# Two fused transformer layers: expert addresses in three VectorE steps with PSUM scratch, unread identity matmuls, and a refitted time table

## The reference, cut to what matters

```python
x  = L0_attn_x                                   # (8, 512, 128)
xn = _layernorm(x)
x  = x + L0_attn(xn) + L0_ffn(xn)                # causal, 16 heads of 8, keys from a latent of 32; routed experts
xn = _layernorm(x)
x  = x + L1_attn(xn) + L1_ffn(xn)                # three attentions mixed (16, 4 and 4 heads); gated dense layers

def _L0_ffn_ref(x, Wg, bg, W1, b1, W2, b2):      # the part that the change touches: 8 experts, the best 2 of a token
    logits = jnp.einsum('bsd,de->bse', x, Wg) + bg
    _, top_idx = jax.lax.top_k(logits, K)
    sel = jnp.sum(jax.nn.one_hot(top_idx, E, dtype=logits.dtype), axis=-2) > 0
    gates = jax.nn.softmax(jnp.where(sel, logits, -jnp.inf), axis=-1)
    for e in range(E):
        h = jax.nn.relu(jnp.einsum('bsd,dh->bsh', x, W1[e]) + b1[e])
        y = jnp.einsum('bsh,hd->bsd', h, W2[e]) + b2[e]
        out = out + gates[..., e:e + 1] * y
    return out
```

## Time and profile before

| | |
|---|---|
| median of 3 runs | 1900.21 us |
| profiled execution: whole / span from first to last instruction | 1906.47 / 1904.7 us |
| busy: TensorE, VectorE, ScalarE, GpSimd | 1548.5, 1290.5, 1038.7, 812.5 us |
| mean granted TensorE clock | 0.898 |
| chain that ended last | PE 52%, DVE 19%, issue 10%, ACT 9%, POOL 4% |
| ScalarE's exponentials waiting for TensorE | 452.2 us in 325 waits, the longest 11.2 |
| step 0 of batches 1 to 7 (start of its maximum) | 181.8, 382.6, 589.2, 804.2, 1019.3, 1234.8, 1449.7 us |

### The profile page before, as it was taken

One profiled execution on the slowest core, in us unless ns is written; L12 is line 12 of the kernel. 1 busy time (PEld: TensorE's weight loads), 2 busy tenths in 40 slices (PEclk: granted clock), 3 DMA queues, 4 the chain that ended last, 5 costly groups with the idle time before them and its releaser, 6 DMA issues.

```text
span 1904.7 us, 34002 instructions
## 1 busy us (share of the span) xinstructions
PE 1548.5 (81%) x11490; PEld 658.2 (35%) x11490; DVE 1290.5 (68%) x3199; ACT 1038.7 (55%) x2258; POOL 812.5 (43%) x728
## 2 busy tenths in 40 slices
PE   2675787988789897998789887998789887988875
PEld 1342442245233542345233542245232542322221
DVE  5645578566886688666985679666885678576523
ACT  2371554666456754666456654666456664645442
POOL 5145446334724455254725446254625443323132
PEclk9985887999899998999899998999898998979876
DMA  5842531144212521134212531135212431010010
GB/s 214 250 118 76 166 102 45 37 113 138 68 37 67 156 80 56 48 103 143 69 37 68 144 91 56 48 100 146 64 41 63 135 100 26 29 39 26 10 34 6
DMA packets 139645, 159.37 MB, mean 84 GB/s; under 512 B 16256, under 2 KB 101072, under 8 KB 138576
## 3 DMA queue, kind: packets, MB, share of 16 engines
q1 hardware_dynamic: 135376, 148.79, 26.4%
q0 software_dynamic: 4096, 8.40, 1.5%
HBM read 115.96 MB, written 40.85 MB: 82 GB/s over the span
## 4 chain that ended last, share of the span: by engine, by line
PE 52%; DVE 19%; issue 10%; ACT 9%; POOL 4%; DMA 3%; SPq 3%; POOLq 0%; ACTq 0%; DVEq 0%
PE banks L434 50%; DVE negmax L825 7%; ACT probs L1165 3%; ACT hm L1234 3%; DVE h L1049 1%; DMA qkc<-relm 1%; SPq L1509 1%; DVE pack L832 1%; DVE r_b L1074 1%; ACT L1165 1%; POOL xslots L1353 1%; DVE xs L984 1%; DVE xn L846 1%; POOL yg L1368 1%; ACT h L1276 1%
## 5 line engine op out<-in xcount | busy, mean ns | idle before, releaser
L1165 ACT ACTIVATE probs<-banks 128x512 f32<-128x512 f32 (+3 forms) x1216 | 582.1, 536 | 475.6 <-PE banks L434 452.2
L825 DVE TENSOR_REDUCE negmax<-banks 128x1 f16<-128x512 f32 x768 | 493.2, 686 | 150.1 <-PE banks L434 145.7
L434 PE MATMUL banks<-kp,qs 32*128 32x512 f16 (+3 forms) x1024 | 242.8, 371 | 126.9 <-DVE negmax L825 77.3
L821 DVE CUSTOM_DVE_ANT_0 scr<-banks,mask_row 128x384 bf16<-128x384 f32 (+3 forms) x512 | 230.1, 487 | 166.7 <-PE banks L434 164.9
L434 PE MATMUL banks<-qs,kp 32*128 32x512 f16 (+3 forms) x1024 | 224.6, 367 | 52.8 <-ACT probs L1165 48.1
L434 PE MATMUL banks<-probs,vp 128*32 128x512 f32 (+3 forms) x2048 | 251.6, 566 | 0.0
L1359 POOL TENSOR_TENSOR hl<-hm,hh 128x512 f16<-128x512 f32 x120 | 139.0, 1158 | 260.3 <-DVE hh L979 260.2
L1379 POOL TENSOR_TENSOR psums<-psums,probs 128x1024 f32<-128x1024 f32 x64 | 149.7, 2362 | 128.1 <-PE banks L434 128.1
L1234 ACT ACTIVATE hm<-banks,wt 128x128 f32<-128x128 f32 x480 | 137.6, 370 | 116.7 <-PE banks L434 116.1
L434 PE MATMUL banks<-qkc 97*128 97x512 f16 (+1 forms) x512 | 173.7, 414 | 24.8 <-DMA qkc<-relm 9.4
L1419 POOL TENSOR_TENSOR h_lo<-h,h_hi 128x512 f16<-128x512 f32 x96 | 112.2, 1185 | 187.7 <-ACT h_hi L1270 95.6
(11 more groups left out here) (207 smaller groups left out, 2531.5 us busy)
## 6 DMA issues: line engine op xcount, KB each, us to landing
wt<-wexp SPq DMA_DIRECT2D x120, 258.0 KB, 2.9
wt<-wexp SPq DMA_DIRECT2D x120, 256.0 KB, 2.7
qkc<-relm SPq DMA_DIRECT2D x96, 128.0 KB
qs<-relq SPq DMA_DIRECT2D x64, 128.0 KB, 2.4
kp<-relk SPq DMA_DIRECT2D x64, 128.0 KB, 2.4
relm<-halves SPq DMA_DIRECT2D x32, 256.0 KB, 2.1
xg<-xslots SPq DMA_DIRECT2D x24, 256.0 KB, 2.9
yslots<-yv SPq DMA_DIRECT2D x24, 256.0 KB, 2.6
```

The costliest lines, as they stand in the source:

```text
L434: return nc.tensor.matmul(psum[rows_, bank, cols_], lhsT, rhs, start=start, stop=stop)
L821: v.tensor_tensor_reduce(scr[:, s, 0:kw], psum[:, SCO + s, 0:kw], mask_row[:, T - kw:T], -1.0, 3e38, ALU.add, ALU.min, negmax[:, g.n % 2, ...
L825: v.tensor_reduce(negmax[:, g.n % 2, c, h:h + 1], psum[:, SCO + s, 0:kw], AX.X, ALU.max, negate=True).then_inc(sem("max"), 1)
L1165: a.activation(keys(g, c)[:, 2 * pair + s, q0:T], psum[:, TRA + s, q0:T], ACT.Exp, scale=SCALE[main(g)]).then_inc(sem("exp"), 1)
```

## The change

1. `slots` is cut in three. `expert_starts` (new, step 53) has the counts and `begin`. `slots` (step 53, was 52) has the rows and `late_f`. `addresses` (new, step 55) has the reductions. `till` and a new `lead` lie in free columns of PSUM bank N, where they were in SBUF. The largest and smallest row are reduced straight into the integer `idx`, and the owner straight into the integer `owner` over seven experts, where a minimum with 7 was taken over eight; so the cast L906, the reduction L907 and the conversion L910 go. The number of VectorE instructions in the chain stays at 14.
2. `turn_over` (new): at steps 72, 6 and 47 TensorE waits for the maximum of the first tile of this step's unit and then writes 6, 3 and 3 matmuls of the identity (128 x 512, 16-bit) into that tile's bank. Nobody reads them. They stand behind `score` and ahead of `trans`. They are left out where the step has no unit: 7, 8 and 7 times, 87 matmuls in all.
3. The time table: `pick` 53 to 56, `add` 53 to 55, the last two gathers 48 and 50 to 48 and 49, `rank1` 46 to 48, which is now behind `rank2` (47), so that the ranks are read before the tie-break is added. The spreads of queries and keys move from steps -11, -10, 1, 14 to -7, -5, 5, 17, the weight stores from -10, -9, 0, 3 to -11, -10, -1, 2. The opening's load and norm come 2 to 3 steps earlier, the first batch's second norm and projections 2 steps (`MOVE` 13 to 11). Most expert steps, and some of the dense layers and of the attentions' ends, move by one or two.

```diff
-      "gex": -32, "gates": -29, "pos": -29, "slots": -28, "pick": -27, "add": 53, "v0a": 3,
+      "xr_lo": -42, ... "rank0": -35, "rank1": -32, "rank2": -33, "gex": -33, "gates": -29,
+      "pos": -29, "starts": -27, "slots": -27, "addresses": -25, "pick": -24, "add": 55, "v0a": 3, "v0a_out": 4, "v0b": 30,
-AT.update({("spread0", i): at for i, at in enumerate((-11, -10, 1, 14), 0)})
+AT.update({("spread0", i): at for i, at in enumerate((-7, -5, 5, 17), 0)})
-AT.update({("gather", c): at for c, at in enumerate((44, 46, 48, 50), 0)})
+AT.update({("gather", i): at for i, at in enumerate((45, 46, 48, 49), 0)})
-AT.update({("w_store", n): at for n, at in enumerate((-10, -9, 0, 3), 0)})
+AT.update({("w_store", i): at for i, at in enumerate((-11, -10, -1, 2), 0)})
+AT.update({("turn", i): at for i, at in enumerate((72, 6, 47), 0)})
...
+        till = psum[:, N, 64:64 + E]
+        lead = psum[:, N, 96:96 + NC * E].rearrange("p (c e) -> p c e", e=E)
...
+                def turn_over(G):
+                    u = UNIT.get(G)
+                    for k, many in enumerate(TURNS):
+                        if u is not None and due(G, ("turn", k)) is not None:
+                            g, j = u
+                            pe.wait_ge(sem("max"), 2 * (8 * g.n + j) + 1)
+                            for _ in range(many):
+                                mm(SCO, slice(0, T), ident16[:, :], ident16[:, :].unsqueeze(1).broadcast_to([P, NC, P]), True, True)
...
-                def slots(b):
+                def expert_starts(b):
                     tri = C("tri").rearrange("p (e f) -> p e f", f=E)
                     full(dve, "n", "pos", b)
                     link(v.tensor_tensor(out=cnt[:, :, :], in0=psum[:, N, NC * E:NC * E + E].unsqueeze(2).broadcast_to([P, E, NC]),
                                          in1=C("steps").unsqueeze(1).broadcast_to([P, E, NC]), op=ALU.is_gt))
-                    link(v.tensor_reduce(till[:, :], cnt[:, :, :], AX.X, ALU.add))
-                    link(v.tensor_tensor(out=cmp1[:, 0, :, :], in0=tri, in1=till[:, :].unsqueeze(1).broadcast_to([P, E, E]), op=ALU.mult))
+                    link(v.tensor_reduce(till, cnt[:, :, :], AX.X, ALU.add))
+                    link(v.tensor_tensor(out=cmp1[:, 0, :, :], in0=tri, in1=till.unsqueeze(1).broadcast_to([P, E, E]), op=ALU.mult))
                     link(v.tensor_reduce(begin[:, :], cmp1[:, 0, :, :], AX.X, ALU.add))
...
+                def slots(b):
+                    link(v.scalar_tensor_tensor(out=lead, in0=per_expert(begin[:, :]), scalar=float(P),
+                                                in1=psum[:, N, 0:NC * E].rearrange("p (c e) -> p c e", e=E),
+                                                op0=ALU.mult, op1=ALU.add))
+                    link(v.tensor_tensor(out=till, in0=till, in1=begin[:, :], op=ALU.add))
+                    v.tensor_tensor(out=first[:, 1, :, :], in0=lead, in1=off[:, :, :], op=ALU.subtract)
+                    v.tensor_tensor(out=first[:, 0, :, :], in0=lead, in1=off[:, :, :], op=ALU.add)
+                    v.tensor_tensor(out=late_f[:, :, :], in0=C("tile")[0:1, :].unsqueeze(2).broadcast_to([1, NT + 1, E - 1]),
+                                    in1=till[0:1, 0:E - 1].unsqueeze(1).broadcast_to([1, NT + 1, E - 1]), op=ALU.is_ge) \
+                        .then_inc(sem("n_taken"), 1)
...
+                def addresses(b):
+                    if b:
+                        dve.wait_ge(sem("gath"), 128 * b)
+                    v.tensor_reduce(idx[:, 0:NC], first[:, 0, :, :], AX.X, ALU.min)
+                    v.tensor_reduce(idx[:, NC:2 * NC], first[:, 1, :, :], AX.X, ALU.max).then_inc(sem("idx"), 1)
...
-                    v.tensor_copy(idx[:, :], best[:, :, :].rearrange("p k c -> p (k c)")).then_inc(sem("idx"), 1)
...
-                    v.tensor_scalar(owner[:, :], cnt[0:1, :, :].rearrange("p e c -> p (e c)")[:, 0:NT + 1], float(E - 1), None, ALU.min) \
-                        .then_inc(sem("owner"), 1)
+                    with nc.allow_low_precision("counts up to seven"):
+                        v.tensor_reduce(owner[:, :], late_f[:, :, :], AX.X, ALU.add).then_inc(sem("owner"), 1)
```

More of the change, by code:

```diff
@@ L74 @@
 LG = LAT + E
+TURNS = (6, 3, 3)
 NT = 15
@@ L80 @@
 A1_AT = (120, 128, 136, 152)
-MOVE = {"front": {}, "prep": {0: 13}, "ca": {-1: -24}, "mid": {-1: -24}, "last": {-1: -30},
+MOVE = {"front": {}, "prep": {0: 11}, "ca": {-1: -24}, "mid": {-1: -24}, "last": {-1: -30},
         "ffn": {-1: -24}, "tail": {-2: -12, -1: -52}}
@@ L130 @@
+AT.update({("spread1", i): at for i, at in enumerate((110, 117, 126, 142), 0)})
 AT.update({("h0", i): at for i, at in enumerate((28, 36, 43, 51), 0)})
@@ L133 @@
 AT.update({("h1_out", i): at for i, at in enumerate((152, 157, 167, 180), 0)})
-AT.update({("up", t): 10 + 2 * t for t in range(NT)})
-AT.update({("down", t): 13 + 2 * t for t in range(NT)})
-AT.update({("wup", t): 6 + 2 * t for t in range(NT)})
-AT.update({("wdn", t): 8 + 2 * t for t in range(NT)})
-AT.update({("scatter", c): at for c, at in enumerate((-27, -26, -25, -24), 0)})
-AT.update({("gather", c): at for c, at in enumerate((44, 46, 48, 50), 0)})
-AT.update({("xg_load", q): at for q, at in enumerate((-22, -21, 8, 16), 0)})
@@ L149 @@
-AT.update({("silu", i): at for i, at in enumerate((134, 136, 138, 140), 0)})
-AT.update({("fb", i): at for i, at in enumerate((134, 136, 138, 140), 0)})
+AT.update({("up", i): at for i, at in enumerate((10, 12, 13, 16, 17, 20, 22, 24, 25, 29, 30, 32, 34, 36, 38), 0)})
+AT.update({("down", i): at for i, at in enumerate((13, 15, 17, 19, 21, 23, 25, 27, 29, 31, 33, 35, 37, 39, 42), 0)})
+AT.update({("wup", i): at for i, at in enumerate((5, 7, 7, 11, 12, 15, 17, 19, 21, 25, 25, 25, 29, 31, 33), 0)})
@@ L151 @@
+AT.update({("fb", i): at for i, at in enumerate((134, 136, 138, 141), 0)})
 AT.update({("glu", i): at for i, at in enumerate((135, 137, 139, 142), 0)})
@@ L892, in slots @@
                     link(v.tensor_reduce(begin[:, :], cmp1[:, 0, :, :], AX.X, ALU.add))
-                    v.scalar_tensor_tensor(out=first[:, 0, :, :], in0=per_expert(begin[:, :]), scalar=float(P),
-                                           in1=psum[:, N, 0:NC * E].rearrange("p (c e) -> p c e", e=E),
-                                           op0=ALU.mult, op1=ALU.add).then_inc(sem("n_taken"), 1)
-                    taken(dve, "n", "pos", b)
-                    link(v.tensor_tensor(out=till[:, :], in0=till[:, :], in1=begin[:, :], op=ALU.add))
@@ L964, in opening @@
                             rank_parts(b, k)
+                    if (b := due(G, "starts")) is not None:
+                        expert_starts(b)
                     if (b := due(G, "slots")) is not None:
                         slots(b)
+                    if (b := due(G, "addresses")) is not None:
+                        addresses(b)
                     if (b := due(G, "gates")) is not None:
```

53 lines of the change are left out of this document (25 added, 28 removed), and 6 rows, old and new, of the table AT.

## The result

| | before | after |
|---|---|---|
| median, us | 1900.1 (1897.2 to 1908.0, 4 runs) | 1764.7 (1761.2 to 1766.5, 4 runs) |
| ratio | | 0.928, interval 0.925 to 0.931 |
| profiled span, us / mean granted clock | 1904.7 / 0.898 | 1764.7 / 0.942 |
| TensorE's idle time, added up over its instructions | 352.8 | 241.7 |
| time at the granted clock of 0.5 | 389.1 | 206.0 |

The change brought 135 us; 51 were forecast, and the range ended at 1815.

The account below looks back on a forecast made before the run. TensorE was taken as the bound, except VectorE at steps 48 to 54. -44 + 7 - 5 - 10 + 1 = -51 from 1906.5 gives 1855.5, and 6.3 less for the median 1849 us; range 1815 to 1885.

Parts of the forecast that it names:

- The chain: Step 52, VectorE: five instructions no longer wait for GpSimd, 7.35 us saved in each of six batches, 44 us.
- 5 us saved once: `add` moved to step 55: no longer blocked by GpSimd's sums in the last batch, 5 us saved; nothing in six others.
- Rival (a): At step 55 `add` takes over the wait for GpSimd's sums, 5.2 us in six batches: 1885 us, chance 0.11.
- rank1: Five instructions moved from step 46 to 48, where VectorE is saturated: 7 us cost, bounds 0 and 7.
- Turns: Unread matmuls at steps 72, 6 and 47 keep TensorE's clock up: 10 us saved, from 5 lost to 36 saved.
- rival (d): The turns' waits for a maximum delay TensorE by 8 us in each of 7 batches: 1915 us, chance 0.04.
- Start: Two weight stores ahead of the first spread: queries and keys 3 us later, first expert's weights 2 us earlier; +1 us.
- The rest of the table: Up, down, sends and `MOVE` shift one or two steps where TensorE sets the pace: nothing, from -8 to +8 us.
- (b): GpSimd becomes the bound around the routing gap and half the chain's saving is lost: 1871 us, chance 0.13.
- The cover: `scatter` waits for step 55 but starts where it did, GpSimd being busy anyway: no cost; failing, 2 to 3 us per batch.
- (c): The clock is healed and `rank1` is hidden, 26 and 7 us more saved: 1816 us, chance 0.18.
- (e): The chain at step 52 stays blocked; only the cost of `rank1` and the turns are left: 1893 to 1900 us, chance 0.03.

Follow-up runs that it names:

- experiment 1: The kernel before with the new chain alone (PSUM scratch, no casts), all at step 52: 1893.1 us, ratio 0.998.
- experiment 4: Two runs on the kernel after: chain back with SBUF scratch, casts and eight experts, 1793.9 us; `add` alone back at step 53, 1811.0 us.
- a_store: The kernel after with the first two weight stores moved behind the first two spreads (steps -4 and -3): 1761.5 us, ratio 0.925.
- a_best: The kernel after with the first two weight stores behind the first two spreads and the second layer's spreads at their old steps: 1765.4 us, ratio 0.928.
- experiment 7: The kernel after with groups of the remaining table entries put back: all 1831.8 us, spreads 1764.8, opening 1772.9; weight stores moved behind the first spreads 1761.5.
- b_ca109: The kernel before with `ca_spread`, the load of `qkc`, at 109 instead of 110 and nothing else: 1891.0 us, ratio 0.993.
- a_sbuf: The kernel after with the chain's SBUF scratch, casts and eight experts given back, the three new steps kept: 1793.9 us, ratio 0.942.

## Why the prediction was wrong

Point by point, by its own steps.

- **The chain.** The mechanism is right: no instruction of it takes over 0.26 us in any batch. The saving on VectorE is 7.5 us per batch (10.1 to 2.6), 7.35 were forecast. What it is worth was off: chain and routing together gave 62 us, where -44, +7 and -5 make 42. Steps 52 to 56 became 9.6 us shorter, not 7.35, more than the 8.5 of the bound. The half clock behind the gap went too, which the prediction had in that bound and did not take.
- **`add`, the failed reasoning within it.** "5 us saved once" priced the move by the only batch where `add` had been seen blocked. In the kernel before the chain shielded `add` in all other batches: it stood under the sums in its place. Without the move the chain's 44 us are 7 by the medians, and not clear of noise (experiment 1), and the kernel after loses 46 (experiment 4). Even the 5 us are not there: in the last batch one instruction of `add` still takes 2.76 us, where it took 5.55. That `add` would start 0.4 us before the sums end was said, and it does (0.47); that this is just late enough in six batches was partly luck. Rival (a) had this mechanism at 5.2 us per batch, and the price is right (7.67 less 2.58 is 5.1), but as something that the change might run into, not as what half of its edits are there to avoid. In all it had 36 us for it, where 46 were measured. That the block goes on from `add` to `pick` was in nobody's sum.
- **`rank1`.** +7 was put down; it was not taken alone. Steps 48 to 52, where it now stands, are 0.9 us longer, about its 1.1. Behind `rank2` nobody reads what it writes: the kernel after leaves out the tie-break and still pays for it. Leaving the five instructions out as well was not tried.
- **Turns.** -10 forecast within +5 to -36; 16 measured in the kernel after, 5 to 7 in the kernel before. Clock 1.0 behind steps 72 and 6 is as said. The slower rival (d) needed 5.9 us of uncovered wait per batch; at step 72 TensorE waited 0.67.
- **Start.** +1 forecast. The stores ahead of the spreads put step 0 at 54.3 us instead of 49.0, not 3 but 5 us later, and moving them behind changes nothing that can be measured (`a_store`). In `a_best` step 0 starts at 48.0 us, and step 0 of batch 1 at 178.5 against 179.2 in the kernel after: batch 0 takes up again what step 0 had gained.
- **"The rest of the table: nothing, from -8 to +8".** This is the step that failed. The forecast missed 84 us, of which chain and routing have some 20, the turns 6, and this step most of what is left. Expert entries, `ca_spread` and opening are worth 23, 63 and 8 us in the kernel after, each taken back by itself. They are not to be added up, since the first two lean on one another (some 11 lost and 9 gained alone, 39 gained together). Put back but for the expert entries, the rest costs 67 us, eight times the bound. `ca_spread` is one of the entries of the attentions that move by one, and neither the prediction nor the description of the change names it.

The reason given for the nothing was that TensorE sets the pace there. It does not in steps 24 to 40 of the kernel before: with nothing but the load moved (`b_ca109`) they fall from 37.0 to 35.3 us. The view of the tile `qkc` in the kernel before says so (by its matmuls alone, TensorE waits 9 us for this load in seven batches):

```profile
  DMA qkc<-relm: 20.5, 16
```

The prediction did not weigh a moved DMA by what SyncE's queue holds ahead of it. It had done this for the spreads at the start, which were worth nothing, and not for `ca_spread`, whose reader comes two steps later.

The rivals: (b) did not come: TensorE's idle time at steps 52 to 55 has no GpSimd in it. But the scatter does not start where it did: it waits 3.20 us for `idx` behind the sums, with VectorE busy. The cover that the prediction gave it failed; no run prices this. (c) had the signs right and too small a sum. (e) is excluded by L915. The forecast gave the rest of the table 8 us either way and no rival gave it more, so the range could not hold the result.

## What to carry to other kernels

A wait that one engine imposes on another's instructions falls on whichever of them stands there: before pricing a cure, list the next instructions of the same kind in that engine's order, and price the cure together with their move.

In a kernel whose order is a written table, price a moved DMA by what waits in the same queue ahead of it at its new place and by how many steps its reader is away; one step can be worth 63 us in 1765. A price of nothing for thirty small edits has to come from the waits of each stretch, not from the share of the busiest engine.

## What the runs showed of the hardware that was not expected

- In most batches one VectorE instruction is held per GpSimd addition, and the next again by the next: three additions of 2.3 us hold three of `add`'s eight (8.08 us for the eight), or three of `pick`'s four (4.01 and 2.36). But one can also be held through several: in the last batch of the kernel before the first of `add` takes 5.55 us, under the rest of one addition and two whole ones. When one is held through several is not known.
- The Trainium skill (SBUF - State Buffer, Who interferes with whom) has it that a VectorE instruction with two SBUF inputs contends with a GpSimd instruction that reads SBUF, and that the ports they share are an exclusive lock. The traces agree: with two SBUF inputs `late_f` took 2.31 us, with one in PSUM 0.25. That the next instruction is caught again, so that the block moves to whatever follows, they show beside it.
- A PSUM operand costs a small VectorE instruction nothing that shows: 0.17 to 0.25 us with it, 0.17 to 0.28 without, where it is not held.
- A reduction over eight experts from 32-bit floats straight into an integer tile takes 0.18 to 0.19 us, as into floats. The separate cast had cost 2.01 under a GpSimd addition, and costs 0.17 where none runs (`a_sbuf`).
- At the start the first two `spread` DMAs behind the 512 KB stores take SyncE's queue 1.24 us each to issue; ahead of the stores, in the kernel before, they took 0.32 to 0.43, and the next two behind them 0.54 and 0.49. The first, in the kernel after:

```profile
47.86 1.24 SPq L1514 DMA_DIRECT2D qs<-relq  x1
```
